# Sums of sparsemax folded once more on GpSimd for the first twenty tiles, and the rest of x put ahead of the reciprocal

## The reference, cut to what matters

```
x = query                                   # 16 x 1024 x 512, float32
# attention over 32 fixed patterns, 16 heads of 32
q = x @ Wq + bq;  k = key_param @ Wk + bk;  v = k @ Wv + bv
z = (q . k) / sqrt(32)                      # for each row and head: 32 scores
p = sparsemax(z)                            # max(z - tau, 0), tau so that p sums to 1
x = layernorm(x + (p @ v) @ Wo + bo)
s = x @ Win + bin                           # 64 columns
h = relu(s[..., None] * W1 + b1)            # 64 x 16
g = sum(h * W2, -1) + b2
out = layernorm(x + g @ Wout + bout)
```

## Time and profile before

| | |
|---|---|
| median of 3 runs | 1354.32 us (1354.13 to 1356.15) |
| the profiled execution | 1352.76 us, its span 1351.0 us |
| TensorE busy | 1251.9 us, 93% of the span |
| VectorE busy | 1138.9 us, 84% |
| ScalarE busy | 1053.6 us, 78% |
| GpSimd busy | 703.2 us, 52% |
| mean granted TensorE clock | 0.967 of full speed |

### The profile page before, as it was taken

The page is one execution under the profiler, slowest core; times in us unless marked ns, Lnnn a source line. Parts: engine busy times, 40 slices in busy tenths (PEclk is TensorE's granted clock), DMA queues, the critical chain, the costliest instruction groups (busy, mean ns, idle before and its releaser), DMA issues. The chain is left out here.

```text
span 1351.0 us, 25359 instructions
## 1 busy us (share of the span) xinstructions
PE 1251.9 (93%) x5838; PEld 867.3 (64%) x5838; DVE 1138.9 (84%) x4573; ACT 1053.6 (78%) x2269; POOL 703.2 (52%) x1674
## 2 busy tenths in 40 slices
PE   7982889999999999999999999999999999899962
PEld 6651666766776776776776776776776777555541
DVE  3977788889999999999999999999998999876764
ACT  2671756688898888899898898888899899666654
POOL 1330333345565555555556555555555556567663
PEclk9995999999999999999999999999999999999975
DMA  6380786555655655655655655655655655668733
GB/s 189 93 210 26 193 231 208 179 171 182 215 189 197 219 192 191 219 193 191 218 192 193 218 192 192 219 196 189 217 195 190 217 196 182 210 231 296 251 94 70
DMA packets 92374, 258.36 MB, mean 191 GB/s; under 512 B 16259, under 2 KB 16259, under 8 KB 75814
## 3 DMA queue, kind: packets, MB, share of 16 engines
q1 hardware_dynamic: 92198, 256.52, 58.7%
HBM read 206.13 MB, written 50.33 MB: 190 GB/s over the span
## 5 line engine op out<-in xcount | busy, mean ns | idle before, releaser
L663 PE MATMUL bank<-G_sb,pT 128*128 128x512 f32 x1024 | 461.1, 593 | 1.9 <-ACT pT L758 1.8
L663 PEld LDWEIGHTS bank<-G_sb,pT 128*128 128x128 f32 x1024 | 185.0, 191 | 185.9 <-issue 183.4
L1077 DVE MAX8 top<-bank 128x8 f32<-128x32 f32 x2048 | 212.3, 179 | 44.5 <-issue 44.5
L466 POOL TENSOR_TENSOR shift_sq<-sum,per_row_sq 128x1 f32<-128x1 f32 x256 | 96.0, 375 | 265.7 <-DVE y_sb L954 263.2
L771 ACT ACTIVATE unread<-y_sb,shift_sq 128x512 bf16<-128x512 f32 x256 | 183.9, 718 | 51.8 <-POOL minus_mean L468 51.7
L1115 DVE SCALAR_TENSOR_TENSOR acc<-hinge,w2c,acc 128x512 f32<-128x512 f32 x224 | 167.4, 748 | 61.7 <-ACT hinge L783 58.3
L783 ACT ACTIVATE hinge<-s_sb,b1c,w1c 128x512 f32<-128x512 f32 x256 | 205.8, 807 | 0.2
L588 PE MATMUL bank<-A_hi,xT_hi 128*128 128x512 f32 x512 | 204.0, 399 | 0.0
L590 PE MATMUL bank<-A_hi,xT_lo 128*128 128x512 f32 x512 | 203.9, 398 | 0.0
L589 PE MATMUL bank<-A_lo,xT_hi 128*128 128x512 f32 x512 | 203.7, 398 | 0.0
L481 POOL TENSOR_TENSOR rstd<-ve,minus_half 128x1 f32<-128x1 f32 x256 | 164.8, 644 | 43.1 <-POOL ve L476 42.8
(11 more groups left out here) (133 smaller groups left out, 2421.9 us busy)
## 6 DMA issues: line engine op xcount, KB each, us to landing
G_sb<-G_of_heads SPq DMA_DIRECT2D x128, 1024.0 KB, 5.4
x_sb<-in_L_attn_query_dram SPq DMA_DIRECT2D x128, 256.0 KB, 4.7
y_sb<-in_L_attn_query_dram SPq DMA_DIRECT2D x256, 128.0 KB, 5.4
out_dram<-o_sb SPq DMA_DIRECT2D x256, 128.0 KB, 4.7
G_of_heads<-y_sb SPq DMA_DIRECT2D x64, 256.0 KB, 3.8
y_sb<-in_L_attn_Wk_dram SPq DMA_DIRECT2D x1, 1024.0 KB, 5.7
y_sb<-in_L_attn_Wq_dram SPq DMA_DIRECT2D x1, 1024.0 KB, 8.2
y_sb<-in_L_attn_Wv_dram SPq DMA_DIRECT2D x1, 1024.0 KB
```

Source lines behind the costliest of these rows:

```text
L466: nc.gpsimd.tensor_tensor(shift_sq[:, par:par + 1], total[:, par:par + 1], per_row_sq[:], ALU.mult).then_inc(s_mean, 1)
L663: mm = nc.tensor.matmul(o_ps[i % 2][:], pT[:, bass.ds(pair_place(turn, i) + (i % H * C + c) * P, P)], G_sb[:, i % GR, c, :], start=(c == 0 ...
L1077: mx = nc.vector.max(top8[:, h, :], z_ps[i % 2][:, h * S:(h + 1) * S])
```

## The change

Early tiles are those with i < EARLY = LAG_WO - LAG_STEP = 20. For them, in slots 3 to 22:

- GpSimd folds side and above twice each, from 32 to 16 and from 16 to 8 elements a head; the second fold waits for the first one's semaphore. VectorE sums over 8 elements a head instead of 16. `folds(i)` gives the semaphore's value after tile i.
- twice is formed on GpSimd (one tensor_scalar of 128 x 16) ahead of its u_sb row. It waits for VectorE's sum_side and for the previous reciprocal.
- VectorE's rest of x (`rest_of_x`) stands ahead of the reciprocal and the step, not behind the step.

For the other 108 tiles twice stays on VectorE, and the subtraction of the step is written as a scalar_tensor_tensor, step * (-1) + u_raw, in place of a tensor_tensor.

```diff
--- before.py
+++ after.py
@@ -248,6 +248,12 @@
         def pool_steps(turn, j):
 
             return isinstance(turn, int) and turn * UNROLL + j < LAG_WO
+
+        EARLY = LAG_WO - LAG_STEP
+
+        def folds(i):
+
+            return i + 1 + min(i + 1, EARLY)
 
         def vector_finishes(turn):
 
@@ -484,11 +490,18 @@
                 nc.gpsimd.tensor_tensor(shift[:, par:par + 1], minus_mean[:, par:par + 1], rstd[:, par:par + 1],
                                         ALU.mult).then_inc(s_shift, 1)
 
-            def fold(s_in, t1, row, s_out):
+            def fold(s_in, i, row, s_out):
 
                 halves = by_head(row[:]).rearrange("p h (a s) -> p h a s", a=2)
-                pool.wait_ge(s_in, t1)
+                pool.wait_ge(s_in, i + 1)
                 nc.gpsimd.tensor_tensor(halves[:, :, 0, :], halves[:, :, 0, :], halves[:, :, 1, :],
+                                        ALU.add).then_inc(s_out, 1)
+
+            def fold_more(i, row, s_out):
+
+                quarters = by_head(row[:]).rearrange("p h (a s) -> p h a s", a=4)
+                pool.wait_ge(s_out, folds(i) - 1)
+                nc.gpsimd.tensor_tensor(quarters[:, :, 0, :], quarters[:, :, 0, :], quarters[:, :, 1, :],
                                         ALU.add).then_inc(s_out, 1)
 
             def slot(turn, j):
@@ -523,6 +536,10 @@
                 if in_range(turn, j, LAG_STEP) and pool_steps(turn, j):
 
                     i = j - LAG_STEP
+                    pool.wait_ge(s_sumc, base + i + 1)
+                    if base + i > 0:
+                        pool.wait_ge(s_inv, base + i)
+                    nc.gpsimd.tensor_scalar(twice[:], sum_side[:], float(S), 2.0, ALU.add, ALU.max).then_inc(s_twice, 1)
                     pool.wait_ge(s_step, base + i + 1)
                     if not isinstance(base, int) or base + i >= UR:
 
@@ -531,8 +548,12 @@
                                             ALU.subtract).then_inc(s_u, 1)
                 if in_range(turn, j, LAG_SIDE):
                     i = j - LAG_SIDE
-                    fold(s_side, base + i + 1, side, s_foldc)
-                    fold(s_above, base + i + 1, above, s_folds)
+                    fold(s_side, base + i, side, s_foldc)
+                    if base + i < EARLY:
+                        fold_more(base + i, side, s_foldc)
+                    fold(s_above, base + i, above, s_folds)
+                    if base + i < EARLY:
+                        fold_more(base + i, above, s_folds)
 
             slots(pool, slot)
 
@@ -896,6 +917,14 @@
         @block.vector
         def _(dve):
 
+            def rest_of_x(i):
+
+                dve.wait_ge(s_xhi, i + 1)
+                nc.vector.tensor_tensor(
+                    xT_lo[:].rearrange("p c n -> p (c n)"), xT_ps[:],
+                    xT_hi[:].bitcast(F32).rearrange("p c n -> p (c n)"), ALU.subtract
+                ).then_inc(s_xlo, 1)
+
             dve.wait_ge(s_const, CONSTS)
             for c in range(C):
                 dve.wait_ge(s_sev, done("kpT") + c + 1)
@@ -954,8 +983,8 @@
                 nc.vector.scalar_tensor_tensor(rows, ps[:], 0.0, other, ALU.add, ALU.add,
                                                accum_out=total).then_inc(s_rows, 1)
 
-            def lower_half(row):
-                return by_head(row[:])[:, :, 0:S // 2]
+            def folded(row, i):
+                return by_head(row[:])[:, :, 0:S // 4 if i < EARLY else S // 2]
 
             def slot(turn, j):
                 base = turn * UNROLL
@@ -971,13 +1000,19 @@
                                             ALU.not_equal).then_inc(s_differs, 1)
                 if in_range(turn, j, LAG_STEP):
 
-                    t1 = base + (j - LAG_STEP) + 1
-                    dve.wait_ge(s_foldc, t1)
-                    nc.vector.tensor_reduce(sum_side[:], lower_half(side), AX.X, ALU.add).then_inc(s_sumc, 1)
-                    dve.wait_ge(s_folds, t1)
-                    nc.vector.tensor_reduce(sum_above[:], lower_half(above), AX.X, ALU.add).then_inc(s_sums, 1)
-                    dve.wait_ge(s_sumc, t1)
-                    nc.vector.tensor_scalar(twice[:], sum_side[:], float(S), 2.0, ALU.add, ALU.max).then_inc(s_twice, 1)
+                    i = base + j - LAG_STEP
+                    dve.wait_ge(s_foldc, folds(i))
+                    if i < EARLY:
+                        dve.wait_ge(s_twice, i)
+                    nc.vector.tensor_reduce(sum_side[:], folded(side, i), AX.X, ALU.add).then_inc(s_sumc, 1)
+                    dve.wait_ge(s_folds, folds(i))
+                    nc.vector.tensor_reduce(sum_above[:], folded(above, i), AX.X, ALU.add).then_inc(s_sums, 1)
+                    if i >= EARLY:
+                        dve.wait_ge(s_sumc, i + 1)
+                        nc.vector.tensor_scalar(twice[:], sum_side[:], float(S), 2.0, ALU.add,
+                                                ALU.max).then_inc(s_twice, 1)
+                if in_range(turn, j, LAG_X) and 0 <= base + j - LAG_STEP < EARLY:
+                    rest_of_x(base + j - LAG_X)
                 if in_range(turn, j, LAG_NORM1):
                     i = j - LAG_NORM1
                     residual(base + i + 1, o_ps[i % 2], s_o, y_sb[:, i % YR, :], s_xr[i % YR],
@@ -1030,17 +1065,12 @@
                         if base + i >= UR:
 
                             dve.wait_ge(s_uT, base + (i - i % GROUP) - UR + GROUP)
-                        nc.vector.tensor_tensor(u_of(i), by_head(u_raw[:, i % 2, :]), spread(step[:]),
-                                                ALU.subtract).then_inc(s_u, 1)
+                        nc.vector.scalar_tensor_tensor(u_of(i), spread(step[:]), -1.0, by_head(u_raw[:, i % 2, :]),
+                                                       ALU.mult, ALU.add).then_inc(s_u, 1)
                 if in_range(turn, j, LAG_SCORE) and not isinstance(turn, int):
                     dve.wait_ge(s_score, base + (j - LAG_SCORE) + 1)
-                if in_range(turn, j, LAG_X):
-                    i = j - LAG_X
-                    dve.wait_ge(s_xhi, base + i + 1)
-                    nc.vector.tensor_tensor(
-                        xT_lo[:].rearrange("p c n -> p (c n)"), xT_ps[:],
-                        xT_hi[:].bitcast(F32).rearrange("p c n -> p (c n)"), ALU.subtract
-                    ).then_inc(s_xlo, 1)
+                if in_range(turn, j, LAG_X) and not 0 <= base + j - LAG_STEP < EARLY:
+                    rest_of_x(base + j - LAG_X)
                 if turn == 0 and j == 1:
 
                     dve.wait_ge(s_wload, 16 * WLOADS)
```

## The result

| | before | after |
|---|---|---|
| median of 17 runs each | 1353.23 us (1351.49 to 1356.15) | 1355.58 us (1353.53 to 1359.25) |
| ratio, with its 95% interval | | 1.0019 (1.0012 to 1.0027) |
| profiled execution / its span | 1352.76 / 1351.0 us | 1356.14 / 1354.4 us |

By the ratio the kernel became slower by 2.6 us (1.6 to 3.7), a little over half of the 4.5 us forecast. The interval leaves no doubt about the direction, but the total doesn't say which terms fell short. The trace has to show that.

What follows compares the result with a forecast made beforehand. TensorE, full from 260 to 600 us, bounds the kernel, so only the filling ahead can shift: 0 + 1.06 + 1.97 + 1.06 + 0.41 = 4.5 us later. Forecast 1358.8 us, range 1352.5 to 1362.5.

Steps and rivals of the forecast that it cites:

- up to X(8): X(j) starts VectorE's rest of x (xT_lo) of tile j, in slot j; X(8) forecast unshifted, 0 (-0.2 to +0.2).
- X(8) to X(9): Check slot 8: 1.32 us lost by the later step, 0.91 won by the nearer next X, 0.41 later.
- X(11) to X(12): Slot ahead of a check: 0.44 us for reciprocal and step before MAX8, 0.2 at the port, 0.65 later.
- X(12) to X(16): Slots 12 to 16, with sorting: 1.32 + 0.65 = 1.97 us later, the 0.91 being no use there.
- 1.32 later, and with it ... MAX8: Check slots: the step moves from 0.38 us before X to 0.94 behind, delaying u_sb, open_any, branch and MAX8 by 1.32.
- rival (a): Check slots: the 2.14 us issue behind open_any runs beside the u_sb wait, the 1.32 falls away; 1353.5 us, chance 0.15.
- Rival (c): TensorE's clock: longer waits at slots 9, 17, 21 bring more half-clock stretches, 1.5 to 4.5 us more; chance 0.08.
- GpSimd's chain: Early slots: from the step's start through u_sb and all folds of side and above, 4.0 us, making the slot 5.25.
- the loop across engines: Early slots: X, score matmul, ScalarE's xT_hi, next X; 5.15 us, below the 5.25 of the loop through GpSimd.
- The port: Slot ahead of a check: the candidates row (L1090) meets GpSimd's second fold of side, 0.2 us lost (0.05 to 0.3).
- Rival (b): Only VectorE's queue counts, reciprocal and step cost nothing in the slot before a check; 1350.9 us, chance 0.12.
- Rival (d): The 108 later tiles: slow scalar_tensor_tensor, 0.55 us more each, nearly all hidden; 1358.8 to 1369 us, chance 0.03.

Runs made afterwards that it cites:

- e7: The changed kernel unaltered, executed once more for a second profile: 1356.45 us.
- e2: The kernel before with only the rest of x moved ahead of the reciprocal for the first twenty tiles, nothing folded: 1360.71 us, ratio 1.0052.
- e4: The changed kernel with the rest of x first only in slots 3 to 6 and the first two behind a check: 1351.96 us, ratio 0.9985.
- e6: The kernel before without the stores of the G pieces, loads of G reading the query instead: 1352.58 us, one execution.
- e5: The kernel before with two VectorE memsets ahead of open_any in check slots 8, 12, 16 and 20: 1355.67 us, one execution.
- e1: The changed kernel with the rest of x back behind the step in all slots, folds and bound staying on GpSimd: 1354.59 us, ratio 1.0.
- e3: The kernel before with only the step subtraction of the 108 later tiles written as scalar_tensor_tensor: 1353.72 us, ratio 1.0.
- e8: The kernel before with the rest of x first in slots 3 to 6 and those leaving 1 or 2 by four, no second folds: 1353.79 us, ratio 0.9993.

## What the prediction had right and what it had wrong

Its terms, against the measured shift in the two executions of the changed kernel (us):

| part of the sum | forecast | after | e7 |
|---|---|---|---|
| up to X(8) | 0 | +0.06 | +0.06 |
| X(8) to X(9) | +0.41 | -0.06 | -0.05 |
| X(9) to X(11) | 0 | -0.02 | -0.02 |
| X(11) to X(12) | +0.65 | +0.53 | +0.51 |
| X(12) to X(16) | +1.97 | +1.22 | +1.66 |
| X(16) to X(20) | +1.06 | +0.90 | +0.92 |
| X(20) to X(21) | +0.41 | +0.01 | +0.01 |
| at X(21) | +4.5 | +2.64 | +3.09 |
| X(21) to X(31) | 0 | -1.53 | -1.53 |

**The direction and the path were right, the size was not.** The step came 0.94 behind X as forecast, open_any 1.32 later, the slot ahead of a check lost 0.53 (0.65 forecast), and e2 shows that this order costs 5.24 us when nothing is folded. Undone only where the sum says that it hurts, it turns the loss into a gain (e4). Set apart from the clock as above, the shift at X(21) is 3.4 us of the 4.5.

**The step that failed is "1.32 later, and with it ... MAX8".** The prediction took the 2.14 us of issue behind open_any as a fixed length that follows open_any wherever it goes. It isn't fixed. MAX8 came 0.84, 0.86 and 0.91 later in slots 8, 16 and 20. The term of 1.32 measured 0.9. That is rival (a) in part: a third of the term ran on beside the wait for u_sb. Two experiments bound the cause. Without the stores of G the distance is as short with open_any in its old place (e6), and with the stores it is as short when open_any comes later (e5, e2, and the changed kernel twice). So the surplus needs both the stores and the early moment. By what the stores hold up the rows behind the branch isn't shown: neither an instruction transfer nor the busy share of the DMA engines sorts the distances.

So the three X(j) to X(j+1) behind a check should go from +0.41 to about -0.05, and two do. The third, X(16) to X(17), has its full +0.41, because VectorE stood idle for 0.48 us there ahead of u_raw, in both executions of the changed kernel (0.50 in e7) and in e2 (0.49); no row shows for what. In that slot what the later branch saved was lost again a few rows on. The other 0.3 us of the gap between 4.5 and 3.4 lie in the slots ahead of a check, X(11) to X(12) and X(17) to X(20), which lost 0.5 each and not 0.65.

**X(12) to X(16).** Forecast 1.97, measured 1.22 and 1.66. TensorE's transposes behind the sorting came 1.50 us later against X(12) (from 94.93 to 125.66 before, from 95.83 to 128.06 after; 1.52 later in e7) where 1.32 was forecast; X(14) to X(16) lost 0.50 and 0.52 where 0.65 was. These two make 2.0. The rest is the clock, which came back sooner behind the sorting and returned 0.77 us (0.37 in e7). That 2.0 meets 1.97 is partly luck: the first distance behind open_any shrank in this slot as well (1.48 to 0.95 us), and an idle time of kind "issue" further on, ahead of the sorting's first row, grew from 0.89 to 1.62.

**The half-clock stretch.** The gain of 1.53 us at X(21) to X(31) was in no term. In the kernel before, TensorE's thirteen score matmuls behind X(21) ran at half clock: from 184.90 to its next transposes at 189.55 are 4.65 us. After, it is 3.11 (187.93 to 191.04), with the clock at 1.00, and X(22) follows X(21) by 5.14 us, not 6.69. The rest ahead of it is 2.07 us in both kernels, so the rest by itself doesn't decide. Of the other traces, e2, e5 and e6 have a stretch of lowered clock there (slot of 6.69 us), e1 and e3 a longer one (7.92 and 7.97), and e4, e7 and e8 none (5.14, 5.15 and 5.52). Rival (c) foresaw more of these stretches and there was one fewer. Whether the change removes it or an execution merely happens to have it stays open.

**The end.** In the full stretch the shift was +1.11 in the profiled execution, +1.56 in e7, and the timed difference is 2.6 (1.6 to 3.7). The profiled span grew by 3.4: 1.11 of the filling, 0.39 ahead of X(0), 1.88 behind X(127). Nothing ties these last two to the change: from X(127) to the end of VectorE's last row it takes 201.9 to 205.0 us in these traces, without a pattern by kernel (203.2 before, 203.8 in e3, 204.1 in e7 against 205.0 after). If the half-clock stretch at X(21) came equally often in both kernels, the filling would give 2.6 to 3.1 us, the shift at X(21), which agrees with the timed 2.6; that is arithmetic, and was not shown.

**Smaller steps.** An early slot of 5.25 us was forecast and found, for another reason. GpSimd's chain was sized at 4.0 from the step and is 3.72 (48.41 to 52.13, where the last fold ends): second folds take 0.42 and 0.45, not 0.50, and follow on their own engine 0.08 after the one before, not 0.17. What binds is the loop across engines, which the prediction put at 5.15 and called the lower one; that both gave 5.25 was luck. The port took 0.05 from the candidates row, the low end of 0.05 to 0.3. The bound on GpSimd takes 0.27 (0.25 taken). Rival (b) fell: the slot ahead of a check did lose its 0.5. Rival (d) fell with e3: 692 ns. The idle time of 0.47 us in slot 7 was in no term. The Trainium skill, Vector Engine (DVE) Microarchitecture Reference, "Points that are easy to get wrong", gives such a row half the throughput; 108 of them here took a median of 692 ns where the tensor_tensor took 692.

**What was not foreseen at all** is how much the port depends on phase. With both parts, the candidates row meets the short second fold of side (0.34 us, above); with either alone it meets the long first fold of above and takes 0.65 in slots 3 to 6, with folds alone as with the order alone. The Trainium skill, SBUF — State Buffer, "SBUF: two separate sides", has a VectorE row with two SBUF inputs and a GpSimd row lock each other out for the whole of an instruction; these rows agree, and the price here is what is left of GpSimd's row when VectorE's arrives: 0.36 us with 0.50 left in e1, 0.05 with 0.18 left in the changed kernel.

## What to carry to other kernels

A row that fills a wait is free only in its place: the step cost nothing ahead of X in a check slot, where VectorE waited for ScalarE anyway, and 1.3 us behind it, where a branch and everything queued behind it waited for it. So choose an order for each kind of slot, by which wait ends last in it, and not one order for all. And an "issue" gap behind a branch is no constant: before adding it to a sum, ask what it stands beside. Here it lost 0.4 to 0.5 us when it came later or when the stores were gone, and in one slot of three the time came back a few rows on. And compare several executions before reading a shift of 1 us: one return of the clock behind a long rest moved by as much with nothing changed.

## What the runs showed of the hardware

- The distance from a read-and-branch to the next row on VectorE is 1.48 to 1.80 us in e6, without the stores. With them it is 1.72 to 2.29 us when the read stands about 1 us behind X, and 1.47 to 1.81 us when it stands 1.7 to 2.35 behind, though the DMA engines can be as busy there (share 0.30 to 1.04, against 0.79 to 0.94).
- VectorE's candidates row of 128x128 took 0.34 or 0.65 us in place of 0.29, by how much of a GpSimd row was left when it began; moving other rows by half a microsecond changed that in slots 3 to 6.
- Behind the sorting, the granted clock of TensorE came back from 0.50 at a moment that differed between executions of one program: the same work took 6.98 and 5.96 us (before and e3).
- TensorE's granted clock fell behind the rest of 2.07 us in one kernel and not in the other; over all traces it fell behind rests of 1.67 to 2.42 us ahead of X(21)'s score, and did not behind rests of 0.83 to 2.08 us.
- Two executions of one filling differ by up to 1.3 us in a slot (7.97 against 6.69), and the ends of the program by up to 3 us, which is more than the change is worth; shifts within the trace, slot by slot, were the better measure.
